# Second routed layer: routing weights by DMA through DRAM, output projection in three fp32r passes, low parts on GpSimd

## The reference, cut to what matters

```python
logits = l2norm(x) @ l2norm(sim_matrix, 0) - sigmoid(gates)
gated = relu(logits)                 # mask: gated > 0, or the best two if none is
probs = softmax(where(mask, gated, -inf))          # [token, 16]: the routing weights
q = sum over e of probs[:, e] * (x @ q_proj[e])    # k and v alike
o = causal softmax attention of one head (q, k, v; 256 tokens a sequence)
y = sum over e of probs[:, e] * (o @ o_proj[e])
```

## Time and profile before

| | us |
|---|---|
| median of the runs | 1845.62 (1844.71 to 1850.81) |
| profiled execution, device time | 1851.05 |
| its span | 1849.2 |
| PE busy | 1545.9 (84%) |
| DVE busy | 1263.7 (68%) |
| ACT busy | 885.1 (48%) |
| POOL busy | 207.6 (11%) |
| layer2_ffn in it | 914 to 1465 |

### The profile page before, as it was taken

One profiled execution on the slowest core, in us unless ns is written; L12 is line 12 of the kernel. 1 busy time (PEld: TensorE's weight loads), 2 busy tenths in 40 slices (PEclk: granted clock), 3 DMA queues, 4 the chain that ended last, 5 costly groups with the idle time before them and its releaser, 6 DMA issues. The chain is left out here.

```text
span 1849.2 us, 26237 instructions
## 1 busy us (share of the span) xinstructions
PE 1545.9 (84%) x8357; PEld 1036.8 (56%) x8357; DVE 1263.7 (68%) x2824; ACT 885.1 (48%) x1615; POOL 207.6 (11%) x200
## 2 busy tenths in 40 slices
PE   6999998886999999988678999999999889756005
PEld 5777765554666665656456566566556455422005
DVE  4988965875677675576565666566655568677985
ACT  3666545763655554655423222322322277537752
POOL 3101012120000000214100000000000111010410
PEclk9999999997999999999989999999999999968557
DMA  4000003210000000521000000000000022000001
GB/s 162 1 1 0 1 1 122 51 43 1 1 1 1 0 1 1 186 55 51 14 1 1 1 1 1 1 0 0 1 1 1 13 68 51 24 0 0 0 0 46
DMA packets 23375, 41.73 MB, mean 23 GB/s; under 512 B 7709, under 2 KB 11165, under 8 KB 22238
## 3 DMA queue, kind: packets, MB, share of 16 engines
q1 hardware_dynamic: 23262, 40.32, 7.4%
HBM read 19.32 MB, written 2.10 MB: 12 GB/s over the span
## 5 line engine op out<-in xcount | busy, mean ns | idle before, releaser
L1012 DVE TENSOR_REDUCE mP_a<-psY_a 128x8 f32<-128x512 f32 x192 | 127.8, 687 | 98.2 <-PE psY_a L838 98.1
L1775 ACT ACTIVATE xsh_f<-xs_f 128x512 fp32r<-128x512 f32 x120 | 75.8, 632 | 198.1 <-DVE xs_f L2028 198.0
L756 ACT ACTIVATE probs_a<-psX_a 128x512 f32<-128x512 f32 x192 | 109.0, 595 | 126.2 <-PE psX_a L865 125.4
L2028 DVE TENSOR_TENSOR xs_f<-xT_f,psR_f 128x512 f32<-128x512 f32 x128 | 86.8, 686 | 78.2 <-PE psR_f L1847 75.1
L1891 PE MATMUL psX_f<-xs_f,wo_f2w 128*128 128x512 f32 x256 | 128.6, 594 | 0.0
L2028 DVE TENSOR_TENSOR xs_f<-aoT_f,psR_f 128x512 f32<-128x512 f32 x128 | 85.8, 684 | 61.7 <-PE psR_f L1847 61.5
L1555 DVE SCALAR_TENSOR_TENSOR g_f<-psU_f,cols_f1w,t_f 128x512 f32<-128x512 f32 (+1 forms) x104 | 77.9, 749 | 72.7 <-ACT t_f L1368 70.8
L2423 PE MATMUL ps_f<-wT_f,xq_f 128*128 128x128 f32 x192 | 24.1, 289 | 122.8 <-DVE xq_f L2444 122.8
L1368 ACT ACTIVATE t_f<-psU_f,cols_f1w 128x512 f32<-128x512 f32 (+1 forms) x104 | 71.1, 684 | 76.5 <-PE psU_f L1434 76.3
L1450 PE MATMUL psO_f<-h_f,w_f1w 128*128 128x512 f32 (+1 forms) x208 | 107.6, 599 | 0.0
L865 PE MATMUL psX_a<-xs_a,ks_a 128*128 128x256 f32 x384 | 85.4, 322 | 13.3 <-ACT xs_a L745 13.3
(11 more groups left out here) (450 smaller groups left out, 4088.7 us busy)
## 6 DMA issues: line engine op xcount, KB each, us to landing
xs_a<-qh_a SPq DMA_DIRECT2D x168, 64.0 KB, 2.0
xs_a<-ql_a SPq DMA_DIRECT2D x84, 64.0 KB, 2.0
xs_a<-probs_a SPq DMA_DIRECT2D x36, 64.0 KB, 2.0
x_sb<-in_x SPq DMA_DIRECT2D x1, 2048.0 KB, 7.9
out<-x_sb SPq DMA_DIRECT2D x1, 2048.0 KB, 6.3
w_f1w<-in_F_w SPq DMA_DIRECT2D x2, 792.0 KB
ctxT<-in_ctxT SPq DMA_DIRECT2D x1, 1024.0 KB, 12.2
maskf_a<-in_mask SPq DMA_DIRECT2D x8, 128.0 KB, 2.2
```

Source lines behind the costliest of these rows:

```text
L756: nc.scalar.activation(probs[:, b % 2, g, :, :], psX[g % 2][:].rearrange("p (e t) -> p e t", e=2), ACT.Exp, scale=float(dv) ** -0.5).then_ ...
L1012: nc.vector.tensor_reduce(mP[:, b % 2, h // 2, col:col + 8], psY[h % 2][:].rearrange("p (h k) -> p h k", h=8), axis=AX.X, op=ALU.max).then ...
L1775: nc.scalar.activation(xsh[:, e % RING, :], xs[:, e % RING, :], ACT.Copy).then_inc(s("x_high").sem, 1)
L2028: nc.vector.tensor_tensor(xs[:, e % RING, :], src, psR[e % 2][:], ALU.mult).then_inc(s("scaled").sem, 1)
```

## The change

The routing weights are transposed as plain fp32 (16 rows), written to DRAM, and read back by DMA with the same row going to all 128 partitions. The four raw weight tensors `wq`, `wk`, `wv`, `wo` are their destination (4 experts each), since all matmuls now take the split weights: `wo` gets high and low parts too, made at the start of the stage. Both stretches and all 16 experts use the same chain: VectorE scales, ScalarE takes the high part, GpSimd the low part, TensorE does three passes. ScalarE's high parts of the O stretch are put between its attention steps. The spreading matmuls, `psR`, `selb`, `three_parts` and `keep_routes` go.

```diff
 layer2_ffn_weights
-    t.update(sim=..., ones=..., sg=..., desc=..., tri32=..., tri=..., self32=sb("self32", [P, E * P]), selb=sb("selb", [P, E * P], BF16))
+    t.update(sim=sb("sim", [P, E]), sg=sb("sg", [P, E]), desc=sb("desc", [P, E]))
...
 layer2_ffn
+    routes = nc.dram_tensor("f2_routes", (ITERS, E * T4), F32).ap()
+        GROUP = 4
+        spread = [wt[k][:].rearrange("p e d -> p (e d)") for k in ("wq", "wk", "wv", "wo")]
+        woh, wol = (ctx.enter_context(nc.sbuf_tensor(n, [P, E, P], F32R)) for n in ("woh_f2", "wol_f2"))
...
+        @block.sync
+        def _(sp):
+            def write(j):
+                sp.wait_ge(gate_parts, j + 1)
+                sp.dma_start(routes[j].rearrange("(e t) -> e t", e=E), rwT[:, j % 2, :])   # routes_kept + 16
+            def read(j, use, g):
+                sp.wait_ge(routes_kept, 16 * (j + 1))
+                if use == 0 and g == 3: sp.wait_ge(o_split, 2)
+                if use: sp.wait_ge(scaled, E * (use - 1) + GROUP * (g + 1))
+                sp.dma_start(spread[g], routes[j, g * GROUP * T4:(g + 1) * GROUP * T4].partition_broadcast(P))
...          # order: write(0), reads of Q 0; then for each j: reads of O j (write(j + 1) before its last), reads of Q j + 1
 gpsimd
+            def low_part(n, e):
+                pool.wait_ge(x_high, n + 1)
+                nc.gpsimd.tensor_tensor(xsl[:, e % RING, :], xs[:, e % RING, :], xsh[:, e % RING, :], ALU.subtract)   # x_split + 1
             def main(j, q):
-                if has_second_next(j):
-                    front(j + 2)
-                keep_routes(j, q)
+                for e in range(E):
+                    low_part(qn(j, e), e)
+                if not is_first(j, 1):
+                    for e in range(E):
+                        low_part(on(j, e), e)
+                        if e == 11 and has_second_next(j):
+                            layernorm_pool(pr, pool, j + 3, w)
+                    if has_second_next(j):
+                        front_norm(j + 2)
+                elif has_second_next(j):
+                    front(j + 2)
             front(0)
+            pool.wait_ge(o_split, 1)
+            nc.gpsimd.tensor_tensor(wol[:], wo[:], woh[:], ALU.subtract)
             front(1)
 scalar
+            def o_high(j, experts):
+                for e in experts:
+                    act.wait_ge(scaled, on(j, e + 1))
+                    nc.scalar.activation(xsh[:, e % RING, :], xs[:, e % RING, :], ACT.Copy)   # x_high + 1
...          # in main, if not first: o_high 0-2 after the copies of q, k, v; 3-4 after two exponentials, 5 after all;
...          # 6-7 before copies 0, 1 of the transposed probabilities, 8-9 before 2, 3; 10-11 before the copy of the
...          # attention output, 12-13 after it; 14-15 after front_squares(j + 2); then store_o(j)
+            nc.scalar.activation(woh[:], wo[:], ACT.Copy)      # before front_squares(1)
 tensor
-            def spread(n, e, weights): ...
 mix_o
-                    pe.wait_ge(scaled, on(j, e + 1))
-                    nc.tensor.matmul(psX[:], wo[:, e, :], xs[:, e % RING, :], start=e == 0, stop=e == E - 1)
+                    pe.wait_ge(x_split, on(j, e + 1))
+                    for m, (wp, xp) in enumerate(((wol, xsh), (woh, xsl), (woh, xsh))):
+                        ins = nc.tensor.matmul(psX[:], wp[:, e, :], xp[:, e % RING, :], ...)
 main
-                    if e == 0: (plain fp32 matmuls of wq, wk, wv with xs)
+                    (all experts: three passes each of q, k, v)
 vector
-            def low_part(j, e): ...
-            front_parts(steps)
             def scale_by(n, use, e, src):
-                dve.wait_ge(gate_bcast, n + 1)
+                if e % GROUP == 0:
+                    dve.wait_ge(spread{e // GROUP}, 16 * (use + 1))
                 dve.wait_ge(hidden, n + 1 - RING)
-                nc.vector.tensor_tensor(xs[:, e % RING, :], src, psR[e % 2][:], ALU.mult)
+                nc.vector.tensor_tensor(xs[:, e % RING, :], src, spread[e // GROUP][:, e % GROUP * T4:(e % GROUP + 1) * T4], ALU.mult)
```

More of the change, by code:

```diff
@@ L1786, in main @@
                 nc.scalar.activation(qkvT[:, 2, :], psQKV[2][:], ACT.Copy).then_inc(s("qkv_ready").sem, 1)
+                if not first:
+                    o_high(j, range(0, 3))
                 for c in range(TPI):
+                    if not first and c == 2:
+                        o_high(j, range(3, 5))
                     nk = P * (c % 2 + 1)
@@ L1791, in main @@
                                          accum_out=rs[:, c:c + 1]).then_inc(s("probs").sem, 1)
+                if not first:
+                    o_high(j, range(5, 6))
                 act.wait_ge(s("vT").sem, s("vT").at(j + 1))
@@ L1842, in out_T @@
                 ins.then_inc(s("ffn_outT_ready").sem, 1)
-            def spread(n, e, weights):
-                pe.wait_ge(s("scaled").sem, s("scaled").at(n - 1))
-                nc.tensor.matmul(psR[e % 2][:], selb[:, e * P:(e + 1) * P], weights, start=True, stop=True)\
-                    .then_inc(s("gate_bcast").sem, 1)
             def v_to_tokens(j):
@@ L1894, in main @@
+                    for m, (wp, xp) in enumerate(((wol, xsh), (woh, xsl), (woh, xsh))):
+                        ins = nc.tensor.matmul(psX[:], wp[:, e, :], xp[:, e % RING, :], start=e == 0 and m == 0, stop=e == E - 1 and m == 2)
+                    ins.then_inc(s("hidden").sem, 1)
             def main(j, q):
-                pe.wait_ge(s("gate_parts").sem, s("gate_parts").at(j + 1))
-                spread(qn(j, 0), 0, rwTb[:, q, :])
-                spread(qn(j, 1), 1, rwTb[:, q, :])
                 for e in range(E):
-                    if e + 2 < E:
-                        spread(qn(j, e + 2), e + 2, rwTb[:, q, :])
@@ L1914, in main @@
+                    for n, (hi_w, lo_w) in enumerate(whl):
+                        for m, (wp, xp) in enumerate(((lo_w, xsh), (hi_w, xsl), (hi_w, xsh))):
+                            ins = nc.tensor.matmul(psQKV[n][:], wp[:, e, :], xp[:, r, :], start=e == 0 and m == 0, stop=e == E - 1 and m == 2)
                     ins.then_inc(s("hidden").sem, 1)
@@ L2059, in mix_o @@
                 for e in range(E):
-                    scale_by(on(j, e), e, aoT[:, q, :])
+                    scale_by(on(j, e), o_use(j), e, aoT[:, q, :])
                     if e in attention:
```

150 lines of the change are left out of this document (82 added, 68 removed).

## The result

The changed kernel takes 1982.2 us (median of 4 runs, 1980.24 to 1984.94), the kernel before 1847.34 (4 runs, 1844.71 to 1850.81): ratio 1.073, 95% interval 1.0704 to 1.0756. It is 135 us slower; the forecast was +93, 1938. In the profiled executions the span grows from 1849.2 to 1983.2 us.

The account below looks back on a forecast made before the run. PE's throughput was taken to set the pace before the change. Terms 8.7 - 3.3 + 1.7 + 73 + 13 = +93 us on 1851.05 gave 1944, forecast as 1938 for the median; own range 1895 to 1975, widened to 1872 to 1990.

Parts of the forecast that it names:

- the main term: Full groups: O 14.4 us longer, 3.9 gained in Q, so 10.5 us longer each; +73 over seven groups.
- rival 3: PE's clock falls too, in O and at the next Q's start; 5 us per group, 1973 us; chance 0.12.
- prologue: Start of the layer: wo's high and low parts delay the first scale; first Q expert ends 8.7 us later.
- group 0: First group, without an O stretch: Q 3.3 us shorter, the turn into group 1 1.7 us longer.
- last O: O stretch alone at the end: 1.08 us per expert becomes 1.83, start 2 us later; +13, bounds +5 and +16.
- The O walk: O stretch: scale, high part, low part, PE follow one another; with the turn 38.5 us for 24.1, +14.4.
- The Q stretch: Q in each group: PE still sets the pace at 2.11 us per expert; gain 3.9 us, bounds 4.2 and 2.
- Rival 1: O stretch: GpSimd's duration alone is the price, engines rarely collide; O near 31, +33, 1879 us; chance 0.13.
- the turn of 2.7 us: From O to the next Q: output store, first high part, low part and semaphores follow one another; 2.7 us.
- Rivals 2 and 4: Whole kernel: PE keeps the pace, 1774 us, chance 0.06; broadcast reads are late, over 2250 us, chance 0.02.
- the upper bound of O: O stretch: 2.6 us per expert through all of O, given as +4.

Follow-up runs that it names:

- filled_pauses: The changed kernel with three bf16 matmuls into a spare PSUM bank ahead of each projection's wait in O; 1978.9 us, ratio 1.069.
- late_store_changed: The changed kernel with ScalarE's copy of the finished projection moved behind the next Q stretch's first high part; 1963.9 us, ratio 1.062.
- the late store: Routing weights by DMA, fp32 output projection, low parts on VectorE, finished projection copied behind next Q's first high part; 1809.5 us, 0.978 of the kernel before.
- late_store_steps: As the late store, with VectorE's routing steps, ScalarE's exponential and the residual addition moved to later experts; 1796.3 us, 0.970 of the kernel before.

## Why the prediction came out as it did

The direction and the mechanism of the main term held; the size was 42 us short. The measured 1982 lies above the forecast's own range (1895 to 1975) and only inside the one widened for the rivals (1872 to 1990); it is nearest to rival 3's 1973. By the prediction's own steps (in the profiled executions; the start of the layer 2.4 us later is no part of the change):

| step | forecast | measured |
|---|---|---|
| prologue, to the end of the first Q expert | +8.7 | +7.4 (29.4 to 36.8 us from the layer's first matmul) |
| from there to O 1's first projection: group 0, Q 1, O's later start | -3.3 + 1.7 - 3.9 + 2.4 = -3.1 | +0.6 |
| six groups, first projection to first projection | 6 x 10.5 = +63 | +99.8 (384.2 to 484.0), 16.6 each |
| last merged O | 14.4 - 2.4 = +12 | +10.5 (21.3 to 31.8) |
| last O with the gap ahead of it | +13 | +10.7 (19.8 to 30.5) |

**The O walk** was nearly right. Its steps counted from PE's last Q work (1208.3): high part 0 begins at 1.6, low part 0 at 2.4, the first projection at 3.7 (forecast 3.9), the first exponential at 9.1 (8.2), projection 7 ends near 21.6 (19), the next Q begins at 41.2 (38.5). Of the missing 2.7 us 0.9 stand there at the first exponential: the scores ran at 1.2 GHz. Where they ran at 2.4 GHz (the fifth O stretch) the first exponential came at 8.0, as forecast; in the other six at 9.0 to 10.3. The other 1.7 us arise up to projection 7, where two normalisations queue behind two low parts, twice a group; I gave each one low part "at least once". The experts of the last O cost 1.69 for the forecast 1.83, and its multiplies (1.76) and low parts (1.66) answer to what was to be seen.

**The Q stretch was the step that failed.** I gave the routing steps 0.2 us, the clock nothing, and took Q at 36.6; it is 40.8. The 2.11 us per expert holds (36.1 for the whole stretch without low parts). What was missing: 2.2 us for the clock (38.6 in the same group with a first expert at 2.4 GHz), and the 2.5 us from there to 36.1, most of them gaps at the routing steps (4.1 us of pauses between passes over 0.5 us apart, against 1.9). That such gaps come from the place of the steps is shown by the later steps, which took them away in the version with VectorE's low parts; in the changed kernel itself this was not tried, and there GpSimd also stretches single steps, 0.22 to 1.17 to 1.27 us. The group shown misses its forecast by 7.0 us, the six on average by 6.1, since the last ones have less beside them; with 3.7 from the first Q stretches, less 5 by which the prologue and the last two O came in cheaper, that is the shortfall in the layer, 35 us. Some 5 more arose outside it. An estimate of the clock's share of the 35: the first exponential came on average 1.5 us later than at full clock in seven O stretches, 10 us, and the six Q stretches that follow an O took 12 us more than 38.6 each (34.6 for the last), which is what they take in filled_pauses and late_store_changed where they start at full clock; together 22.

**Rival 1** (GpSimd's duration alone) fell: contention alone costs 75 us. But waiting costs as much, and the exclusion of O's scales by itself costs only 15; which of the other VectorE instructions in the merged O stretch carry how much was not separated further. **Rival 3** was more right than its chance of 0.12: the clock fell in both places and cost 2.2 us in a Q and 1.6 to 2.7 us in most O stretches, against the 5 us per group that it named. It should have been a term of the sum, since the turn of 2.7 us that I had worked out stood beside a row with a pause of 3.7 us followed by a clock of 0.81. **Rivals 2 and 4** fell with the waits on GpSimd and with the hidden reads. The lower end of the forecast's range, 1895, does not follow from its own bounds, which add up to 8.7 - 3.3 + 1.7 - 7 x 0.5 + 5 = +9, 1854; nor does the upper bound of O, since 2.6 us per expert from a first projection at 3.9 through the turn make 45.6 us, +7 and not +4. The outcome lay above both, so neither decided it.

## What to carry to other kernels

Before a step is handed to an idle engine, ask who waits for it and where its partner's operands lie: 120 low parts on GpSimd in the Q stretches, beside scales with one input in PSUM, cost the layer 0.2 us, and 256 in both stretches, beside scales with both inputs in SBUF and at the end of a chain that PE waits for, cost it 154. The place of the operand alone is a small part of that: putting it right in O gave 15. A throughput gain on the engine that sets the pace is paid out only if its suppliers keep their lead: after the spreads had gone, moving one 0.6 us copy and five small steps was worth more (32 us) than the change from spreads to DMA itself (26). A pause that one adds ahead of dense matmuls is to be priced twice, once for itself and once for what may run at half clock behind it, above all where a chain of other engines waits for it, as for the scores here. And a mean clock that rises says nothing of the place that matters: fillers lifted O's from 0.73 to 0.96 and left the scores at 3.0 us.

## What was not expected of the hardware

The turn into one Q stretch is longer than its neighbours in many of the kernels, and it is the one where the loop starts its second round: 1.67 us against 1.31 before, 2.75 against 0.42 with the late store, 5.28 against 2.0 with all low parts on VectorE. In the kernel after and in those without low parts, with unawaited ones, with aoT in PSUM and with fillers it is not longer. In late_store_steps it is VectorE that is late. Its first scale of the long turn, and that of the next turn:

```profile
1161.38 1.29 DVE L2035 TENSOR_TENSOR xs_f<-xT_f,wq_f2w 128x512 f32<-128x512 f32 x2 [2.67 <-PE psX_f L1910]
...
1218.84 1.29 DVE L2035 TENSOR_TENSOR xs_f<-xT_f,wq_f2w 128x512 f32<-128x512 f32 x2
```

VectorE is idle for 2.67 us before the first and for nothing before the second, though the read of its weights had landed at 1151.3. Why it is late there these traces don't show.

With the late store in the changed kernel, the clock behind the short turn was sometimes full and sometimes half, in the same program: first nine passes of 2.20, 2.21, 3.41, 3.68, 3.98 and 2.31 us after pauses of 0.96, 0.95, 1.91, 0.95, 0.64 and 0.81. And in the late-store version a pause of 2.75 us was followed by 2.21, in the one with later steps a pause of 2.76 by 3.73. The pause alone doesn't decide it; what does, these runs don't show.
